# Interaction-network tower on one core: B loads moved to ScalarE's queue, A, C and stores tile by tile, x1 of a tile's first unit in mid-slot, gathers one by one

## The reference

```python
def _cin_forward(X0, Ws):            # X0: (1024, 24, 16); W0: (24*24, 64), W1, W2: (24*64, 64)
    F_ = X0.shape[1]
    Xk = X0
    outs = []
    for W in Ws:
        H_prev = Xk.shape[1]
        Wr = W.reshape(F_, H_prev, W.shape[1])
        Xk = jnp.einsum('bfd,bhd,fho->bod', X0, Xk, Wr)
        outs.append(Xk.sum(axis=2))
    return jnp.concatenate(outs, axis=1)
h = jnp.concatenate([z, dense_ctx], axis=1)      # 192 + 16
h = jnp.maximum(h @ W_top1 + b_top1, 0.0)        # 512
h = jnp.maximum(h @ W_top2 + b_top2, 0.0)        # 256
y = h @ W_top3
```

## Time and profile before

| | |
|---|---|
| runs of the kernel before | 423.25 us median of 3 (416.54 to 425.3) |
| the profiled execution | 421.92 us, span 420.1 us |
| PE, DVE, ACT, POOL busy | 342.1, 288.5, 189.7, 233.2 us |
| DMA queue of SP / of the gathers | 74.2% / 3.2% of 16 engines' span |
| bytes moved by DMA | 73.63 MB, mean 175 GB/s |

### The profile page before, as it was taken

How to read it: one execution, slowest core, us unless ns; L and a number is a source line. 1 busy time by engine, 2 the same in 40 slices (tenths; PEclk the granted TensorE clock), 3 DMA queues, 4 the chain that set the end, 5 groups by cost and what they waited for, 6 DMA issues and landing times.

```text
span 420.1 us, 6106 instructions
## 1 busy us (share of the span) xinstructions
PE 342.1 (81%) x2296; PEld 150.5 (36%) x2296; DVE 288.5 (69%) x277; ACT 189.7 (45%) x346; POOL 233.2 (55%) x252
## 2 busy tenths in 40 slices
PE   0045899438396969599999997999999999999997
PEld 0043422102041323244333433543444344443466
DVE  2001499129385959578987998798899999898700
ACT  1000026113335345273737573757556475745374
POOL 5775888888888888788788887677400000000000
PEclk9998899859886999999999999999999999999999
DMA  3355936499799998999799979998999799731000
GB/s 101 74 111 116 231 83 157 83 231 234 164 242 233 252 257 152 228 231 213 163 228 223 232 137 222 233 235 163 225 251 266 156 251 258 214 107 44 2 2 2
DMA packets 59263, 73.63 MB, mean 175 GB/s; under 512 B 31489, under 2 KB 36609, under 8 KB 59234
## 3 DMA queue, kind: packets, MB, share of 16 engines
q1 hardware_dynamic: 53090, 71.66, 74.2%
q0 software_dynamic: 6144, 1.59, 3.2%
HBM read 48.05 MB, written 1.58 MB: 118 GB/s over the span
## 4 chain that ended last, share of the span: by engine, by line
PE 68%; DMA 10%; issue 9%; POOL 3%; another core or an unknown queue 2%; ACT 2%; SPq 2%; DVE 1%; DVEq 0%; ACTq 0%
PE ps_x L370 44%; PE ps_tower L370 9%; PE ps_turn L370 6%; PE ps_b L370 5%; POOL x_rows L191 3%; DMA A<-x_scratch 3%; DMA B_sb<-x_sb 2%; DMA x_scratch<-x_rows 2%; PE ps_turn L415 2%; PE ps_turn L423 1%; SPq L256 1%; DMA C<-x_scratch 1%; DVE Z L337 1%; PE ps_tower L376 1%
## 5 line engine op out<-in xcount | busy, mean ns | idle before, releaser
L347 DVE TENSOR_TENSOR Z<-A,ps_b 128x1024 f32<-128x1024 f32 x192 | 222.0, 1214 | 29.5 <-remote 18.8
L191 POOL DMA_INDIRECT x_rows<-tbl,ids_sb x192 | 190.8, 994 | 62.6 <-issue 43.6
L370 PE MATMUL ps_x<-Z,w_sb 128*64 128x512 f32 x768 | 188.4, 609 | 1.7 <-issue 1.0
L337 DVE TENSOR_TENSOR Z<-A,C 128x1024 f32<-128x1024 f32 x48 | 58.1, 1224 | 75.5 <-DMA C<-x_scratch 37.4
L370 PEld LDWEIGHTS ps_x<-Z,w_sb 128*64 128x64 f32 x768 | 50.3, 139 | 84.3 <-issue 65.8
L370 PE MATMUL ps_x<-Z,w0s_sb 128*64 128x512 f32 x192 | 48.3, 626 | 24.4 <-DVE Z L337 23.9
L635 ACT ACTIVATE x_diag<-ps_turn,mask_sb 128x192 f32<-128x192 f32 x128 | 50.6, 606 | 9.9 <-PE ps_turn L423 9.8
L618 ACT COPY ps_b<-B_sb 128x1024 f32<-128x1024 f32 x45 | 46.4, 1030 | 9.8 <-DMA B_sb<-x_sb 5.9
L648 ACT COPY G<-ps_turn 128x416 f32<-128x416 f32 x31 | 15.7, 506 | 73.5 <-remote 45.8
L599 ACT COPY x_sb<-ps_x 128x512 f32<-128x512 f32 x16 | 9.4, 586 | 78.2 <-PE ps_x L370 78.2
L204 POOL MEMSET pause_sb<- 128x768 f32 x56 | 42.3, 756 | 3.6 <-DMA x_scratch<-x_rows 3.6
(11 more groups left out here) (48 smaller groups left out, 147.2 us busy)
## 6 DMA issues: line engine op xcount, KB each, us to landing
A<-x_scratch SPq DMA_DIRECT2D x48, 512.0 KB
B_sb<-x_sb SPq DMA_DIRECT2D x90, 256.0 KB
C<-x_scratch SPq DMA_DIRECT2D x32, 512.0 KB
x_rows<-tbl,ids_sb POOLq DMA_INDIRECT x192
x_quarters<-x_scratch SPq DMA_DIRECT2D x16, 96.0 KB
x_scratch<-x_rows SPq DMA_DIRECT2D x7, 192.0 KB
w_sb<-w SPq DMA_DIRECT2D x2, 384.0 KB
C<-x_scratch SPq DMA_DIRECT2D x2, 256.0 KB
```

What stands on the lines that cost most here:

```text
L191: pool.indirect_dma_start(out=x0_rows[t % 2][:, f * D:(f + 1) * D], out_offset=None, in_=tables[f], in_offset=bass.IndirectOffsetOnAxis(ap ...
L337: nc.vector.tensor_tensor(Z[s % ZR][:, :], A[u % AS][i][:, :], C[u % 2][i][:, :], ALU.mult).then_inc(z_ready, 1)
L347: nc.vector.tensor_tensor(Z[s % ZR][:, :], A[u % AS][i][:, :], ps_b[j % 2][:, :], ALU.mult)\
L370: return nc.tensor.matmul(out, lhsT, rhs, start=start, stop=stop)
```

## The change

`load_b` moves from SP to ACT, and is issued right behind `copy_x1` (in even slots in three pieces, in odd ones and in slots 0 to 2 in one). SP now does store(t), C, A and quarters of both units of a tile, and then the next store. `x1_at` becomes 6 in odd slots and slot 2, 12 in slot 1 (behind all its products), and stays 0 in even slots from 4 on. `copy_c` of a tile's first unit moves ahead of `copy_b(u, 2)`; `sum_x1` moves to product 1 of the next slot; tower pieces move by a few products, two of them ahead of a slot's first product. Before every gather there is now a memset of 288 columns, and the gathers don't wait for products any more.

```diff
 RB = 8
-PAUSE = 768
+PAUSE = 288
...
 
 def x1_at(u):
 
-    return NP2 // 2 if u < 2 else 0
+
+    return NP2 if u == 1 else NP2 // 2 if u % 2 == 1 or u < AS else 0
 
 
 def made_x1(u, i):
...
-                    after(pool, z_ready, PER_SLOT * (2 * t - 5) + 2 * PER_SLOT * f // F)
                     gather(t, f, gathered[t % 2])
 
         @block.sync
...
-            def load_b(u, k):
-
-                j = k + 1
-                if k == 0:
...
-            for u in range(2, UNITS):
-
-                if u == 2:
-                    for k in range(NJ - 1):
-                        load_b(u - 1, k)
-                    store_tile(1)
-                if u % 2 == 0:
-                    wait_stored(sp, u // 2)
-                sp.wait_ge(z_ready, made_x1(u - 2, NI - 1))
-                for i in range(NI - 1):
-                    load_c(u, i)
-                for i in range(NI):
-                    if u >= AS:
-                        sp.wait_ge(z_ready, made_x2(u - AS, NP2 - NI + i))
-                    load_a(u, i)
-                if u > 2:
-                    for k in range(NJ - 1):
-                        load_b(u - 1, k)
-                if u % 2 == 1 and u + 1 < UNITS:
-                    store_tile((u + 1) // 2)
-                sp.wait_ge(x0_turned, u - 1)
-                load_quarters(u)
-                if u == W - 1:
+            for t in range(1, TILES):
+
+                store_tile(t)
+                wait_stored(sp, t)
+                for u in (2 * t, 2 * t + 1):
+                    sp.wait_ge(z_ready, made_x1(u - 2, NI - 1))
+                    for i in range(NI - 1):
+                        load_c(u, i)
+                    for i in range(NI):
+                        if u >= AS:
+                            sp.wait_ge(z_ready, made_x2(u - AS, NP2 - NI + i))
+                        load_a(u, i)
+                    sp.wait_ge(x0_turned, u - 1)
+                    load_quarters(u)
+                if t == 1:
...
-            for k in range(NJ - 1):
-                load_b(UNITS - 1, k)
...
-                for n in range(NP2):
+                for n in range(NP2 + 1):
                     if n == x1_at(u) and u + 1 < UNITS:
                         for i in range(NI):
                             cross1(u + 1, i)
-                    cross2(u, n)
-                    if n == x1_at(u) + 4 and u + 1 < UNITS:
-                        sum_x1(u + 1)
+                    if n < NP2:
+                        cross2(u, n)
+                    if n == 1 and u > 0:
+                        sum_x1(u)
...
-                if w == 0 and n in (8, 9, 10):
-                    at = 4 * (n - 8)
+                if w == 0 and n in (6, 8, 9):
+                    at = 4 * (6, 8, 9).index(n)
                     sum_z3(g, range(at, at + F // 6))
-                if w == 1 and n in (1, 5, 8):
-                    sum_h1(g, (1, 5, 8).index(n))
+                if w == 1 and n in (-1, 5, 8):
+                    sum_h1(g, (-1, 5, 8).index(n))
...
-                if (w, n) == (3, 1):
+                if (w, n) == (3, -1):
...
                     pe.wait_ge(tower_in, 16 * 8)
+                if g > 0:
+
+                    tower(g - 1, w, -1)
...
                         turn_x0(u)
-                        if u + 1 < UNITS:
-                            make_b(u + 1, 0)
+                    if n == (8 if x1_at(u) else 7) and u != 1 and u + 1 < UNITS:
+                        make_b(u + 1, 0)
                     if g > 0:
                         tower(g - 1, w, n)
+                if u == 1:
+                    for i in range(NI):
+                        cross1(u + 1, i)
+                    make_b(u + 1, 0)
 
...
 
+            def load_b(u, k):
+
+                j = k + 1
+                act.wait_ge(x1_copied, u + 1)
+                if u > 1:
+                    act.wait_ge(b_copied, (NJ - 1) * (u - 2) + k + 1)
+                for q in range(2):
+                    src = x1_sb[u % 2][H * q + j:H * (q + 1):NJ, :].unsqueeze(1)
+                    nc.scalar.dma_start(B_sb[k][:, HALF * q:HALF * (q + 1)], src.to_broadcast([HR, FR, HALF]))\
+                        .then_inc(b_in[k], 16)
+
...
                     copy_x2(u - 1)
-                if 2 <= u < UNITS - 1:
+                first = x1_at(u) == 0 and u + 1 < UNITS
+                if first:
                     copy_x1(u + 1)
+                    load_b(u + 1, 0)
                 if u > 0:
                     copy_x2_rows(u - 1)
                     copy_b(u, 1)
+                if first:
+                    load_b(u + 1, 1)
                 if towers and w == 1:
                     relu_h1(g - 1, 0)
                 if towers and w == 2:
...
                     copy_g(u - 1, 0)
+                    if x1_at(u) == NP2 // 2 and u + 1 < UNITS:
+                        copy_c(u + 1)
                     copy_b(u, 2)
+                    if first:
+                        load_b(u + 1, 2)
                     copy_g(u - 1, 1)
-                if u == 1:
-                    copy_c(2)
-                if u < 2:
+                if x1_at(u) == NP2 // 2 and u + 1 < UNITS:
...
                     copy_x1(u + 1)
-                elif u + 2 < UNITS:
-                    copy_c(u + 2)
+                    for k in range(NJ - 1):
+                        load_b(u + 1, k)
...
                     copy_y(g - 1)
+                if u == 1:
+                    copy_c(2)
+                    copy_x1(2)
+                    for k in range(NJ - 1):
+                        load_b(2, k)
+                if u > 1 and u + 2 < UNITS and x1_at(u + 1) == 0:
+                    copy_c(u + 2)
                 if u + 1 < UNITS:
                     copy_b(u + 1, 0)
-                if u == 1:
-                    copy_c(3)
 
             act.wait_ge(mask_in, 16)
```

More of the change, by code:

```diff
@@ L35 @@
 WARM = (40, 16, 16, 4)
-BURST = 3
+BURST = 1
 PER_SLOT = NI + NP2
 def x1_at(u):
-    return NP2 // 2 if u < 2 else 0
+    return NP2 if u == 1 else NP2 // 2 if u % 2 == 1 or u < AS else 0
 def made_x1(u, i):
```

## The result

The changed kernel takes 443.88 us (median of 4 runs, 437.77 to 446.54) against 421.06 for the kernel before beside it: ratio 1.053, 95% interval 1.029 to 1.076. It is slower by 5%, where 421 us and no change were forecast. Ratios here compare only executions within 1.5% of the fastest of their kernel, and the one profiled then (446.54 us) was the slowest of the four. The holes stand in the same places in both traces of the changed kernel, and are longer in the first.

The account below looks back on a forecast made before the run. PE was taken to set the pace at the stream's end, with start waits and unexplained late sums among gathers before it. The terms summed as 421.9 - 6 + 5 + 0 = 421 us, range 404 to 432.

Parts of the forecast that it names:

- B on ACT's queue: Odd slots: six B issues in a row make ACT late for PE's x2; 7.5 us reckoned, +5 us taken.
- Slot 1: Start: slot 1's products run through before x1 of unit 2, B lands sooner, x2 is turned earlier; -6 us.
- Gathers: Single gathers with a short pause run at 1.57 us against 1.50 each; taken as 0, bounds +3 and some -20.
- late sums: Among gathers, a slot's second sum G reaches ACT up to some 5 us late; assumed to go with the gathers' running.
- A, C and stores tile by tile: SP no longer waits for x1 and ACT's copies between loads; 0, with 0 to -2 us.
- even to odd slots: Cross1 products in mid-slot no longer hide the x2 copy; a tower piece replaces them, up to 0.7 us in slot 3; 0.
- slower: Outcome over 431.7 us, most of rival 2 and a little of the forecast's upper side; chance 0.18.
- Rival 1: Slots 2 to 10: single gathers free the sums G; 409 us, or 404 with ACT's issues hidden; chance 0.29.
- Rival 2: Odd slots 3 to 13: B, issued in mid-slot, lands too late for x2; 434 us; chance 0.20.
- Rival 3: DMA engines are the bound with the same bytes to move, so the start's gain is given back; 423.6 us; chance 0.1.

Follow-up runs that it names:

- e3: Changed kernel with the B loads of even units back on SP, odd units' B staying on ACT: 410.26 us, 0.993 of the kernel before.
- e6: The changed kernel, unchanged, run and traced again: 435.42 us median, 1.054 of the kernel before; the traced execution took 431.57 us.
- e4: Changed kernel with the copies of C in odd slots moved ahead of the copy of x1: 430.19 us, 1.041 of the kernel before.
- e5: The kernel before, unchanged, run for a second profile on the same chip as e6: 411.02 us.
- e7: e3 with the gathers of the kernel before (three in a row, long pause, waits for products): 409.94 us, 0.993 of the kernel before.
- e8: Kernel before with only its B loads moved to ACT, in pairs behind copies (in slots 0 and 1 in a row): 413.83 us, ratio 1.002.
- e2: Changed kernel with the gathers of the kernel before (three in a row, pause of 768 columns, waits for products): 442.32 us, ratio 1.068.
- e1: Kernel before with only the change's gathers (single, pause of 288 columns, no wait for products): 418.36 us, ratio 1.011.
- e9: Changed kernel with the six B issues of odd slots from 3 on spread behind x1 and later copies: 424.71 us, 1.003 of the kernel before.
- e15: e3 with the copies of C ahead of the copy of x1 in odd slots, on the chip of e13: 427.80 us, 0.996 of the kernel before.
- e12: The kernel before, unchanged, traced for the third time, on the chip of e13 and e15: 425.56 us.
- e13: e3 unchanged, run again on another chip: 424.63 us, 0.990 of the kernel before.

## Why the prediction was wrong

**The step that failed is "B on ACT's queue", +5 us (7.5 reckoned): it was 21 to 23 us.** The mechanism was the one named, six issues in a row on ACT ahead of the copy of x2, but its price and its deadline were wrong, and what a hole costs in clock was left out.

- *PE's side was right.* From the copy of x1 to the turning of x2 I reckoned 10.4 us of PE's own work. In e3, without the issues, these are 10.2 us in slot 5 (190.59, the copy, to 200.8).
- *The issues were mis-sized.* Six took 4.6 to 6.1 us in the odd slots from 5 on in e6, 5.3 on average, and up to 7.45 in the profile after, not 3.6 (six by the median of SP's 0.60). Of the two rows of SP's own one had six at 4.81 us, 0.80 each, the other at 3.75: the rows were there, and I multiplied a median, which gives less than either. So ACT's chain from x1 to x2 took 13.2 us in slot 5 of e6 (189.41 to 202.61), not 12.0.
- *Two deadlines were missed.* I measured ACT's chain at its end, the copy of x2. But the copies of C stand in it, and behind them come a product of DVE and one of PE before PE may turn x2. From the end of C to the turning are 2.4 us in slot 5 of e3 (198.4 to 200.8) and 2.5 in e6 (201.1 to 203.6), while ACT needs only 1.5 from there to the end of the copy of x2. This is 1 us more. In slot 5 that makes 14.2 us from x1 to the turning, 4.0 more than in e3, where I had 1.6. In slots 7 and 11 this is the wait that PE shows, 3.7 and 3.6 us.
- *The other one is the tower's activation.* In slots 5, 9 and 13 it stands right behind the issues, and PE's next piece of the tower waits for it. PE in slot 5 of e6:

```profile
195.74 0.65 PE L348 MATMUL ps_tower<-z_dense,wt1a_sb 80*64 80x256 f32 x4 [2.23 <-ACT h L670]
...
196.66 4.44 PE L348 MATMUL ps_x<-Z,w_sb 128*64 128x512 f32 x12
200.93 2.75 PE L348 MATMUL ps_x<-Z,w0s_sb 128*64 128x512 f32 x12
203.60 0.66 PE L393 MATMUL ps_turn<-id_sb,x_sb 128*128 128x128 f32 x4
```

  The wait of 2.2 us, and 12 matmuls at 4.4 instead of 2.7 behind it, are 3.9 of the 4.0 us, and PE has no gap at the three products behind them, so here either deadline alone gives the loss. Slot 9 is the same (3.2 us of wait, 12 matmuls at 4.3), and slot 13 has both waits, 1.7 for the activation and 1.3 for the product. It fits e4, where C alone was freed: slots 5 and 9 gained 0.2 us or lost by it.
- *The clock was left out.* A hole lowers it: behind that of slot 7 the matmuls ran at the lower of the two levels, 1.2 GHz. In e6 it was 0.92 in two of the five pairs (0.96, 0.96 and 1.00 in the others), in e5 0.96 in one and 1.00 in four. In e3 it is 1.00 in all five. At slot 7, 4 matmuls and the turning took 3.1 us instead of 1.6.

Those five odd slots lost 4.0, 4.3, 4.9, 4.8 and 3.3 us, where the prediction had 1.6, 1.0, 1.6, 1.0 and 1.6.

**Slot 1, -6 us: wrong by its size too.** DVE did run its twelve products through, and in the trace after cross1(2) ended at 97.8, as reckoned. But the first quarter of B was used 11.3 us after its first issue in e6 (11.6 in the profile after), not 7.5:

```profile
98.23 0.58 ACT L584 COPY x_sb<-ps_x 128x512 f32<-128x512 f32 x1 [7.91 <-PE ps_x L348]
98.84 3.79 ACTq L604 DMA_DIRECT2D B_sb<-x_sb  x6
110.09 1.02 ACT L614 COPY ps_b<-B_sb 128x1024 f32<-128x1024 f32 x1 [11.27 <-DMA B_sb<-x_sb]
```

The own queue brought nothing: the upper bound, B behind A and C, is what came, and e3, which issues the same six from SP, used the quarter 9.5 us after the first. So x2(1) was turned at 111.7, 2.9 us earlier than in e5, and not 5.95, and at x2(4) 0.2 us were left. Where the rest went is open. A gather took the 1.57 us reckoned (47.37 to 48.94 in the trace after), and tile 2, which I had left out, was stored at 119.7 in e6 and 113.4 in e5; but e7, where it is stored 3.2 us earlier than in e3, has x2(4) no earlier. (A slip in the same sum: 107.5 + 1.0 + 0.6 is 109.1, not 109.3.)

Here the rule of the Trainium skill decides as the prediction had it ("DMA: Bandwidth & Descriptors", "Issuing engines are not separate DMA queues"): DMAs of several engines interleave on the same 16 engines, and a second issuer saves only the time to initiate them, "which is usually small relative to the DMA itself". The trace agrees on the first half: B took 11.3 us on its own queue, and e8 shows a ratio of 1.002. As to the second: the time to initiate six was 5.3 us on average in the odd slots, and on an engine with due work behind it this time, with the clock lost by the holes, was the loss.

**Gathers, 0: right in the new order** (e7 against e3: equal; e2 with the old form 1.068, the change 1.054), and 1% slower in the old one (e1). The reason that I gave, late sums, was wrong: see below. **A, C and stores tile by tile, 0; even to odd slots, 0**: not tried alone; e3, which has both, comes out at 0.993, 3 us faster with all the rest in it, which bounds their sum and not each.

**The rivals.** Rival 1 (single gathers free the sums G) can't account for a slower kernel, and with e1 and e2 there were no late sums to free; by itself it was not tried on a chip that has them. Rival 2 (B lands too late in odd slots) gave the sign and somewhat over half the size, 434, by the wrong cause (and its sum took off 7.5 us of ACT's chain, of which the forecast held only 5: its own terms give 437): from slot 5 on ACT waits for no B load in e6; the five waits (18.9 us, longest 11.3) all lie before 158 us. Rival 3 (the DMA engines, 423.6 us) fell: e3 moves the same bytes in less time than the kernel before. The prediction put "slower" at 0.18, most of it on rival 2; no rival was ACT's chain costing more than the 7.5 us reckoned.

## What to carry to other kernels

When instructions are put in front of others on an in-order engine, list all that stands behind them and who waits for each, on every engine, and follow the one that is wanted first to the common end; a deadline in the middle of the chain with another engine's work behind it can come before the one at its end. Price a run of DMA issues by a run of them in the trace, not by the median of one, and put them behind instructions that are already queued, where they issue beside the engine's work, not behind one on which the engine has just waited. A slip of a few microseconds on TensorE is also paid in clock: 1.5 us here behind one of 3.7.

The best order found is e3: the even units' B on SP, 0.993 and 0.990 of the kernel before on two chips (0.990 to 0.995 and 0.983 to 0.997).

## What the runs showed of the hardware

- **A run of issues is dearer than its median says.** ACT's 90 issues in e6 have a median of 0.622 us, and its 18 pairs take 1.19 to 1.97 us, 0.68 an issue on average; the nine runs of six take 3.79 to 6.08 us, 0.84 an issue, with single ones up to 2.08. What makes some long was not tried.
- **Late sums come with the chip, or its condition.** On the two chips where the kernel before took 414 us, none of the eight traces (e1 to e8) has a wait of ACT for a sum G whose signal fits no recorded matmul ("remote" below). On the other two, where it took 428 to 429, all seven (e9 to e15) do, as does the first trace of the kernel before. The same program, the waits of ACT for G (us in total, times, longest), in e5:

```profile
ACT G L648 <- PE ps_turn L370: 31.4, 29, 2.7
ACT G L648 <- issue: 1.7, 1, 1.7
```

and in e12, where "remote" means that no recorded instruction ended at the signal:

```profile
ACT G L648 <- remote: 51.3, 15, 6.1
ACT G L648 <- PE ps_turn L370: 21.7, 16, 2.5
```

Their spans are 409.2 and 423.8 us. Other signals of PE are late in e12 as well (31 such waits in all, 87 us), and none once the gathers are over. With single gathers and e3's order on that chip, the "remote" waits for G are 3.8 us in 2 (e13) and 16.2 in 5 (e15, with C early), and others stay, 38 us in all in e13. Yet e13's span is 14.3 us above e3's on the other chip, just as e12's is 14.6 above e5's. So fewer late signals did not make the kernel lose less by them, and the cause of the lateness stays open. It hardly touches the ratios to the kernel before on the same chip, e3's being 0.993 on one and 0.990 on the other, but a time from one chip can't be held against one from another here.
